# Combine and the last attention layer in one pipeline of 16 groups, K and Q masked by ScalarE from PSUM, and the context's LayerNorm in the routing stage

## The reference, cut to what matters

```
# block 0
x = LN1(x + attention(x, x, causal))              # 16 heads of 8
x = LN2(x + attention(x, ctx))
p = softmax(x @ router_w + router_b)              # 8 experts, the best 2 are kept, top-2 softmax weights
x = LN3(x + sum_of_2(weight * expert(x)))         # expert: gelu(x @ w1 + b1) @ w2 + b2, FF = 512
# block 1
qn = LN(x, ln1); kn = vn = LN(ctx, ln1)
x = x + attention(qn, kn, vn)                     # not causal
x = x + gelu(LN(x, ln2) @ w1 + b1) @ w2 + b2
```

## Time and profile before

| | us |
|---|---|
| median of 3 runs (lowest, highest) | 1588.02 (1587.35, 1588.13) |
| profiled execution, its time | 1589.83 |
| its span, first to last instruction | 1588.0 |
| TensorE busy | 1270.0 (80%) |
| VectorE busy | 974.7 (61%) |
| ScalarE busy | 982.6 (62%) |
| GpSimd busy | 877.4 (55%) |
| mean granted TensorE clock | 0.886 of full |

### The profile page before, as it was taken

One profiled execution on the slowest core, in us unless ns is written; L12 is line 12 of the kernel. 1 busy time (PEld: TensorE's weight loads), 2 busy tenths in 40 slices (PEclk: granted clock), 3 DMA queues, 4 the chain that ended last, 5 costly groups with the idle time before them and its releaser, 6 DMA issues. The chain is left out here.

```text
span 1588.0 us, 60533 instructions
## 1 busy us (share of the span) xinstructions
PE 1270.0 (80%) x23136; PEld 1060.0 (67%) x23136; DVE 974.7 (61%) x2203; ACT 982.6 (62%) x2016; POOL 877.4 (55%) x1392
## 2 busy tenths in 40 slices
PE   5999999899999863979999990212149999994998
PEld 2778777778888752879999990111127777773776
DVE  4677777678787706935555543666537777762332
ACT  1778787788888700956666661545537777762554
POOL 2467676666767520089999867777323545432331
PEclk9999999999999955989999995555559999996999
DMA  3323333232222140012222223565422222211221
GB/s 97 89 86 93 104 94 101 83 89 85 85 81 79 36 134 0 0 51 69 66 69 68 66 62 104 155 172 152 134 86 82 81 85 89 83 42 48 73 66 54
DMA packets 161789, 130.76 MB, mean 82 GB/s; under 512 B 18208, under 2 KB 131360, under 8 KB 161696
## 3 DMA queue, kind: packets, MB, share of 16 engines
q1 hardware_dynamic: 153248, 112.20, 23.7%
q0 software_dynamic: 8448, 17.32, 4.7%
HBM read 86.93 MB, written 42.47 MB: 81 GB/s over the span
## 5 line engine op out<-in xcount | busy, mean ns | idle before, releaser
L753 DVE TENSOR_REDUCE at_mx<-at_ps_s 128x16 f32<-128x1024 f32 x128 | 155.9, 1219 | 108.5 <-PE at_ps_s L491 62.2
L684 ACT ACTIVATE at_pt<-at_ps_t 128x1024 f32<-128x1024 f32 x128 | 130.6, 1020 | 54.5 <-PE at_ps_t L505 53.7
L1445 POOL DMA_INDIRECT ex_xg<-x,ex_ti x136 | 148.0, 1088 | 23.4 <-issue 21.8
L677 ACT ACTIVATE at_pr<-at_dd 128x1024 f32<-128x1024 f32 x128 | 135.1, 1056 | 34.6 <-DVE at_dd L761 34.5
L1505 ACT ACTIVATE ex_hg<-ex_ps_h,ex_wt 128x128 f32<-128x128 f32 x544 | 154.5, 373 | 1.2 <-PE ex_ps_y L1474 1.2
L761 DVE TENSOR_TENSOR at_dd<-at_ps_s,at_mx 128x1024 f32<-128x1024 f32 x128 | 153.4, 1200 | 0.1
L1526 DVE COPY ex_wt<-experts 128x1156 f32 x136 | 104.8, 772 | 75.3 <-DVE ex_y L1532 73.0
L1655 POOL DMA_INDIRECT cb_yg<-rows,cb_sl x128 | 124.6, 973 | 47.0 <-issue 45.7
L1465 PE MATMUL ex_ps_h<-ex_xt,ex_wt 128*128 128x128 f32 x1088 | 147.8, 279 | 0.0
L505 PE MATMUL at_ps_t<-ident,at_pr 128*128 128x128 f32 x1024 | 140.0, 280 | 5.6 <-issue 4.3
L1474 PE MATMUL ex_ps_y<-ex_wt,ex_hg 128*128 128x128 f32 x1088 | 143.7, 275 | 0.5 <-ACT ex_hg L1505 0.5
(11 more groups left out here) (239 smaller groups left out, 3279.3 us busy)
## 6 DMA issues: line engine op xcount, KB each, us to landing
rows<-ex_y SPq DMA_DIRECT2D x136, 64.0 KB
x<-at_ln_out SPq DMA_DIRECT2D x32, 256.0 KB, 3.2
at_kx<-in_xt SPq DMA_DIRECT2D x16, 256.0 KB, 2.8
at_qx<-in_xt SPq DMA_DIRECT2D x16, 256.0 KB, 2.8
at_vin<-in_xt SPq DMA_DIRECT2D x16, 256.0 KB, 2.8
at_xr<-in_x SPq DMA_DIRECT2D x16, 256.0 KB, 3.1
x1t<-at_xt SPq DMA_DIRECT2D x16, 256.0 KB, 3.3
at_kx<-in_ctxt SPq DMA_DIRECT2D x16, 256.0 KB, 2.8
```

The source lines that it names most:

```text
L677: act.activation(pr[:, p], dd[:, p], ACT.Exp, scale=SCALE).then_inc(p_ready, 1)
L684: act.activation(pt[:, 2 * h + p], ps_t[:, :, :, :], ACT.Copy).then_inc(pt_ready, 1)
L753: dve.tensor_reduce(mx[:, p], ps_s[:, :, 4 * p:4 * p + 4, :], AX.X, ALU.max).then_inc(mx_ready, 1)
L1445: pool.indirect_dma_start(out=xg[:, s, :], out_offset=None, in_=x_src, in_offset=bass.IndirectOffsetOnAxis(ap=ti[:, s:s + 1], axis=0)).the ...
```

## The change: what it does

1. A new `fused_phase` replaces `combine_phase` and the second `attention_phase`. A group passes first through the combine steps (called the front here) and then through attention, one to four steps later, while other groups are in the other parts. Its tiles are still named `l_`. The normalised x is no longer stored transposed and loaded again: TensorE transposes `z4` into `ps_g` (`turn_z`), and ScalarE copies it to `qx`. x itself is stored and, for the residual, loaded again. The context is loaded once for K and V (`kv`).
2. K and Q: ScalarE writes `kb` and `qb` directly from PSUM, two activations each with a per-partition scale (0 or 1) and a bias that is masked beforehand. The copies `kt`, `qt` and GpSimd's masking are gone. `kb`, `qb`, `vx` and `ot` exist twice.
3. 1/std in the front comes from GpSimd's power operation, as elsewhere in the kernel, on 8 columns at once (`front_rstd`). ScalarE's square root and the Newton step are gone.
4. The context's LayerNorm, transposes and stores move to the routing phase: all 16 groups of the context are loaded first (256 KB each), normalised in place by VectorE, GpSimd and ScalarE in four parts of four groups, transposed by TensorE, copied over the transposed tokens, and stored. The experts' weights are loaded behind them. VectorE's three operations on the weights (line 1080 before) come later, just ahead of the one-hot loop.
5. `vx` and three small constants are larger.

```diff
+            def _(act):          # fused_phase, ScalarE
+                def mask_k(a):
+                    act.wait_ge(k_ready, a.g + 1)
+                    if beyond(a.g, 1):
+                        act.wait_ge(s_ready, 2 * a.g - 2)
+                    for j in range(2):
+                        ins = act.activation(kb[:, a.u, j, :], ps_g[:, :], ACT.Identity,
+                                             bias=side[:, 0, 2 + j:3 + j], scale=c.side[:, 2 + j:3 + j])
+                    ins.then_inc(kb_ready, 1)
...
+                def scale_own(a):
+                    act.wait_ge(fnb_ready, a.g + 1)
+                    if beyond(a.g, 1):
+                        act.wait_ge(zg3_ready, a.g - 1)
+                    front_scale(z3[:, a.u], fy[:, a.u], a, OWN).then_inc(z3_ready, 1)
...
+            def _(dve):          # fused_phase, VectorE
+                def step(a):
+                    g = a.g
+                    if a.exists():
+                        maximum(g * 2 + 1, 1)
+                    if a.shift(-1).exists():
+                        recip(g * 2 - 1, 1)
+                    if a.shift(3).exists():
+                        weigh_second(a.shift(3))
+                    if a.exists():
+                        subtract(g * 2 + 1, 1)
+                    if a.shift(3).exists():
+                        own_statistics(a.shift(3))
+                    if a.shift(-1).exists():
+                        normalise(a.shift(-1), 1)
+                    if a.shift(3).exists() or a.shift(2).exists():
+                        front_moments(a.shift(3))
...
+            def _(pool):         # fused_phase, GpSimd
+                def step(a):
+                    g = a.g
+                    if a.shift(3).exists():
+                        fetch(a.shift(3), 0, 1)
+                        fetch(a.shift(3), 1, 2)
+                        fetch(a.shift(3), 2, 3)
+                    if a.shift(-2).exists():
+                        spread(g * 2 - 3, 1)
...
 def route_phase: TensorE
                     mm = pe.matmul(ps_l[:, t, :], xt[:, P * t:P * t + P], c.rw[:, :], start=True, stop=True)
                 mm.then_inc(lg_ready, 1)
+                def turn_context(g):
+                    pe.wait_ge(zc_ready, g + 1)
+                    if g > 1:
+                        pe.wait_ge(zct_ready, g - 1)
+                    for t in range(GP):
+                        tr = pe.transpose(ps_c[g % 2][:, P * t:P * t + P], cx[:, g, t, :], c.ident[:, :])
+                    tr.then_inc(tc_ready, 1)
+                for g in range(NG // 2):
+                    turn_context(g)
                 pe.wait_ge(both_ready, 1)
...
 def route_phase: ScalarE
+                for g in range(NG - NG // CB):
+                    scale_context(g)
                 act.wait_ge(work_ready, 1)
                 act.activation(w["ex"][:, :, :], w["sh"][:, :, :], ACT.Exp).then_inc(exp_done, 1)
+                for g in range(NG - NG // CB, NG):
+                    scale_context(g)
+                for g in range(NG // 2):
+                    copy_context(g)
                 act.wait_ge(work_ready, 2)
...
 def build
-        combine_phase(nc, c, r, "cb_", x2, rows, d["ctx"], x3, z3t, ctxzt)
-        attention_phase(nc, c, "l1_", [
-            Layer(c, "l1", z3t, ctxzt, x3, x4, None, False, None, None, True, False)])
+        fused_phase(nc, c, r, "l1_",
+                    Layer(c, "l1", None, ctxzt, x3, x4, None, False, None, None, True, False), x2, rows, x3)
```

More of the change, by code:

```diff
@@ L33 @@
 HB = 4
+CB = 4
 W1, B2 = 0, FF
@@ L936, in route_phase @@
+def route_phase(nc, c, r, tag, xt, experts, ctx_src, ct_out):
     with ExitStack() as ctx:
@@ L994, in _ @@
                     [P, E, D])).then_inc(r.loaded, 16)
+                for g in range(NG):
+                    sp.wait_ge(zct_ready, g + 1)
+                    sp.dma_start(ct_out[:, GT * g:GT * g + GT], xt[:, GT * g:GT * g + GT]).then_inc(zc_stored, 16)
+                sp.wait_ge(zc_stored, 16 * NG)
             @block.tensor
@@ L1004, in _ @@
                 pe.matmul(ps_tot[:, :, :], ones[:, :], w["both"][:, :, :], start=True, stop=True).then_inc(rank_ready, 1)
+                for g in range(NG // 2, NG):
+                    turn_context(g)
                 def hot(b, s, first, last):
@@ L1050, in _ @@
                                          ALU.mult, ALU.add))
+                for h in range(CB):
+                    dve.wait_ge(in_c[h], 16 * (NG // CB))
+                    for g in range(NG // CB * h, NG // CB * h + NG // CB):
+                        for t in range(GP):
+                            ins = dve.bn_stats(cstats[:, g, t, :], cx[:, g, t, :])
+                    ins.then_inc(cstats_ready, 1)
+                    dve.wait_ge(cstats_ready, h + 1)
+                    dve.memset(ctick[:, :], 0.0)
+                    for g in range(NG // CB * h, NG // CB * h + NG // CB):
+                        for t in range(GP):
+                            ins = dve.bn_aggr(cmv[:, g, t, :], cstats[:, g, t, :])
+                    ins.then_inc(cmv_ready, 1)
                 dve.wait_ge(lg_ready, 1)
@@ L1121, in _ @@
                 dve.tensor_copy(r.expert[:, :], expf[:, :])
+                dve.wait_ge(exp_done, 2)
+                linked(dve.tensor_scalar(v["den"][:, :], v["ed"][:, :], 1.0, None, ALU.add))
+                linked(dve.reciprocal(r.weight[:, 0, :], v["den"][:, :]))
+                dve.tensor_tensor(r.weight[:, 1, :], v["ed"][:, :], r.weight[:, 0, :], ALU.mult)
                 def hot(b, s, first, last):
@@ L1152, in _, with flat @@
                                    pattern=[[1, P]], channel_multiplier=-1).then_inc(made, 1)
+                for h in range(CB):
+                    part = slice(NG // CB * h, NG // CB * h + NG // CB)
+                    wide = NG // CB * GP
+                    def flat(a):
+                        return a[:, part, :].rearrange("p g t -> p (g t)")
+                    pool.wait_ge(cmv_ready, h + 1)
+                    pool.tensor_tensor(flat(cneg), cmv[:, part, :, 0].rearrange("p g t -> p (g t)"),
+                                       c.minus_one[:, 0:wide], ALU.mult)
+                    pool.tensor_tensor(flat(cvar), cmv[:, part, :, 1].rearrange("p g t -> p (g t)"),
+                                       c.eps[:, 0:wide], ALU.add).then_inc(cvar_ready, 1)
+                    pool.wait_ge(cvar_ready, h + 1)
+                    pool.tensor_tensor(flat(crstd), flat(cvar), c.minus_half[:, 0:wide], ALU.pow).then_inc(
+                        crstd_ready, 1)
+                    pool.wait_ge(crstd_ready, h + 1)
+                    pool.tensor_tensor(flat(cnb), flat(cneg), flat(crstd), ALU.mult).then_inc(cnb_ready, 1)
         n.clear()
@@ L1849, in build @@
     x2 = scratch("x2", (T, D))
[L1850 removed]
+    x3 = scratch("x3", (T, D))
     x4 = scratch("x4", (T, D))
```

854 lines of the change are left out of this document (567 added, 287 removed).

## The result

The kernel after takes 1459.49 us (median of 4 runs, 1456.18 to 1463.04), the kernel before 1588.08 us (4 runs): ratio 0.9186, 95% interval 0.9174 to 0.9198. It is 128.6 us faster. The forecast was 1447 in a range of 1427 to 1488, that is 141 us faster: direction and mechanism were right, the gain was 12 us smaller. The profiled execution took 1463.04 us with a span of 1461.3, 14.9 over the forecast's span of 1446.4; it was the slowest of the four, 3.5 us over the median.

The account below looks back on a forecast made before the run. VectorE was to bound the fused loop at 17.2 us a group, the step taking 17.8. From a span of 1588.0, -148.6 for the fused phase and +7 for routing gave 1446.4, so 1447 us; 8-in-10 range 1427 to 1488.

Parts of the forecast that it names:

- VectorE as the bound, 17.2 us a group: Fused loop: VectorE has the most work a group, 11.6 us from attention plus 5.6 from combine, 17.2 in all.
- The step of 17.8: Fused loop: one full step takes 17.8 us, between 17.2 without stalls and 20.5; 13 such steps make 231 us.
- 3 us of clock reserve: Start of the fused loop's full steps: 3 us added until TensorE's clock is up.
- the masked write was taken at 0.64: ScalarE in the fused loop: each of four masked writes takes 0.64 us, within 0.59 to 0.8; ScalarE needs 16.1 a group.
- The two margins "under 0.3 us": Fused step: ScalarE's scaling before `gain_own` and TensorE's second scores finish under 0.3 us before VectorE wants them.
- GpSimd: 8 fetches and the power: GpSimd in the fused loop: 8 fetches 10.2 us, power with small operations 1.7; 15.4 to 16.4 a group in all.
- Start of the phase: Fused phase: beginning runs at GpSimd's pace; VectorE's first mixed step ends 58.5 us after the phase starts.
- Routing: Routing phase with the context's work added: +7 us, between +3 and +12; exponential +2.8, ranks +6.2 containing it.
- (a): Rival, fused loop: VectorE's two-input SBUF operations hold up GpSimd, step up to 20.5 us, time 1482; chance 0.21.
- (b): Rival, fused loop: front and attention do not overlap, 26.8 us a step, time 1564; chance 0.05.
- (c): Rival, fused loop: TensorE never gets full clock, 31 us a step, time 1619, slower than before; chance 0.02.
- The signs named: Loop: VectorE over 93%, steps 17.2 to 18.8 us, GpSimd and ScalarE over 85%, clock near 1.00; routing: ranks near 625.

Follow-up runs that it names:

- e6: Kernel after with the head of TensorE's fused-phase loop placed on the start of a 256-instruction code block: 1436.9 us, ratio 0.9063 to the kernel before.
- e11: e6 with VectorE taking the statistics of each group's sum twice, into a tile nobody reads: 1446.0 us, ratio 0.9105 to the kernel before.
- e8: e6 with half of the row sums' matmuls left out in the fused phase, so its result is not the reference's: 1428.4 us, ratio 0.9002.
- e12: e6 with one more masked write of K a step on ScalarE, into a tile nobody reads: 1440.5 us, ratio 0.9084 to the kernel before.
- e10: e9 with VectorE's subtraction that frees the scores' bank moved ahead of the second weighted sum: 1431.4 us, ratio 0.9018.
- e9: e6 with, in routing, the ranks ahead of all context transposes and the exponential after 8 scaling groups instead of 12: 1435.4 us, ratio 0.9036.

## Why the prediction was right, and where it was off

**VectorE as the bound, 17.2 us a group: right.** The step is 17.3 to 17.5 in the kernel after before its first jump, 17.35 in e6, and e11 shows it from the other side; e8's 17.0 shows that 0.35 us of the 17.35 hang on TensorE. With TensorE's code kept the fused order lets VectorE run through at 98%.

**The step of 17.8: this term was mis-sized.** Its mean was 19.1 over twelve steps. The prediction sought the loss in handovers and in VectorE's hold on GpSimd, and both were smaller than it allowed (17.35 where TensorE's code is kept). The cause was in none of its steps or rivals: it counted TensorE's matmuls, 15.2 + 0.55 us, but not its instructions. The loop of the kernel before is kept with one step a pass; that the change has two was to be had from the diff (`over_single` against `over_steps`), and the length of a step from the trace of before. The text ahead of the prediction has all loops in two groups; TensorE's in the attention phase was the exception. In the kernel after the four jumps between residual 0 and 12 lengthen their steps by 3.7 to 5.2 us each, the pause at 1190.62 its step by 3.1. e6 removes both for 20.4 us and lands at 1436.9, ten under the forecast; in its span, 11.9 under the forecast's, the stretch from the first full step to the last residual has 8.4 of them (272.6 us against 281: 13 x 0.45 us and the 3 us of clock reserve that were not needed), and 3.3 lie before routing, where nothing was changed.

**ScalarE: the masked write was taken at 0.64 from start to start, it took 0.67.** The raw `l_kt` of 0.69, with a bias, became 0.775 with a scale as well: 85 ns. The four are 0.1 us a step more; e12 shows that ScalarE had room for more than that. The two margins "under 0.3 us" were therefore too pessimistic; in e6 VectorE waited 1.4 us in 160 for the scores and not once for ScalarE. `load_kv` was hidden, as counted: TensorE's waits in the loop name no transfer.

**GpSimd: 8 fetches and the power.** The power took 1.02 us on 4 columns, 1.67 on 8 and 2.91 on 16, between the two bounds. But in e6 GpSimd was busy 110.4 of 160 us, 69%, and with the 14.9 us between its fetches 78%; over 85% was forecast.

**Start of the phase: right,** 58.3 us against 58.5. The 3 us for the clock were not needed: it is 0.50 from 1015 to 1021 us, 0.95 from 1021 to 1025 and 1.00 behind that.

**Routing: right in sum, +7.0, in part by luck.** Its terms differ: the exponential +3.9 (forecast 2.8), since the scalings started 2.7 us later than assumed, 1.9 of them the power on 16 columns; the ranks +5.3 (6.2), the token list +4.7 with the weights' operations in it, where +7 was forecast. Another 2.3 us came behind it, in the experts phase (first tile +0.8, the run of 136 tiles +1.4), which no step foresaw and whose cause is open.

**Rivals.** (a) exists at about a tenth of its price: the fetch takes 0.98 us beside VectorE's work, and of GpSimd's other operations `rcx` alone meets a two-input operation of VectorE in every step, once; e10 values that at 0.31 us against 2.7. The two do not merely slow each other: one waits for the other (0.70 to 0.76 us in place of 0.34). That is shown for this pair alone. The prediction read it on the fetches, not on `rcx`. (b) and (c) did not occur. The clock of 0.94 in the loop follows TensorE's pauses: it is 0.79 from 1127 to 1135 us, right behind the pause that ends at 1125.9, 1.00 from 1135 to 1160, and 1.00 throughout this stretch in e6. The argument against (c), that a stretch busy without a pause has clock 1.00, does not hold as it stands: the first line of the earlier trace rows has TensorE busy 24.85 of 26 us at 0.50.

**The signs named:** VectorE over 93% and steps of 17.2 to 18.8 us held only in the undisturbed stretch; from 1085 to 1250 us ScalarE was busy 80% and GpSimd 67%, where over 85% was said. The ranks came at 625.04 where 625 was said (1.2 us of that lie before routing), the first subtraction 49.6 us after the phase's start, the masked writes lie within 0.6 to 0.8, and `gain_own` waited once, for 0.2 us.

## What to carry to other kernels

When a change makes a loop's body longer, count the engine's instructions as well as their time, and look at the instruction queue in the loop before and after: packets that repeat with each pass (9 here, none in e6) mean that the code isn't kept, and an idle marked "issue" at the first instruction of the body (3.3 us here) is its price. Laying the loop's head on a block's start, or the hint on its jump, is a change of a few words and was worth 20 us here. In a pipeline that one engine bounds, adding a known operation to each engine in turn shows in two runs which one it is and how much room the others have.

## What the runs showed of the hardware

- TensorE's body of 1662 instructions was brought in again in 9 packets of 16 KB a pass where its place was left open (kernel after), and kept when it began on a block's start (e6: no packet in four passes). The jump back took 3.7 to 3.9 us when it was not kept and 0.22 when it was.
- On the first chip of the experiments, kernels whose TensorE code is brought in ran more slowly: steps of 21 to 29 us where another took 17.4 to 22.9, with a kept loop at exactly the same 15.44 us on both. Its runs also scatter more (the kernel before 1602 to 1625 us, against 1583 to 1592).
- VectorE's weighted sum (128x128) and GpSimd's product `rcx` (128x256) waited for each other in e9: 0.70 to 0.76 us in place of 0.34 for the sum, 0.74 in place of 0.61 for the product.
- GpSimd's power operation: 1.02, 1.67 and 2.91 us for 4, 8 and 16 columns of 128 partitions.
